# Layer 1's attention scores from half-height stacks on two ranges of rows, and eight maxima of the third group moved to the end of the front

## The reference, cut to what matters

```python
xn = _layernorm(x, axis=-1)
q = _rope(xn @ Wq, cos, sin); k = _rope(xn @ Wk, ...); v = xn @ Wv
k = jnp.repeat(k.reshape(B, S, Hkv, hd), 4, axis=2)     # one key head for four query heads
scores = jnp.einsum('bhqd,bhkd->bhqk', q, k) / jnp.sqrt(jnp.float32(D))
p = jax.nn.softmax(scores, axis=-1)
o = jnp.einsum('bhqk,bhkd->bhqd', p, v)
x = x + o.transpose(0, 2, 1, 3).reshape(B, S, D) @ Wo + slot_ffn(xn)
```

## Time and profile before

| | us |
|---|---|
| median of 3 runs (lowest, highest) | 3282.1 (3274.93, 3283.18) |
| the profiled execution | 3282.72 |
| its span | 3281.0 |
| PE busy | 3021.9 (92%) |
| DVE busy | 1858.9 (57%) |
| ACT busy | 1339.0 (41%) |
| POOL busy | 313.7 (10%) |

### The profile page before, as it was taken

One profiled execution on the slowest core, in us unless ns is written; L12 is line 12 of the kernel. 1 busy time (PEld: TensorE's weight loads), 2 busy tenths in 40 slices (PEclk: granted clock), 3 DMA queues, 4 the chain that ended last, 5 costly groups with the idle time before them and its releaser, 6 DMA issues.

```text
span 3281.0 us, 49871 instructions
## 1 busy us (share of the span) xinstructions
PE 3021.9 (92%) x14086; PEld 1839.2 (56%) x14087; DVE 1858.9 (57%) x4528; ACT 1339.0 (41%) x1921; POOL 313.7 (10%) x349
## 2 busy tenths in 40 slices
PE   5999999999989999999989999999997789989998
PEld 2455545554445555555545555556665466666666
DVE  5655665666547777777637767752223644444552
...
GB/s 205 136 108 80 161 145 107 72 161 148 44 81 49 49 60 61 55 61 55 72 176 32 51 40 37 45 61 76 95 59 66 105 72 91 91 91 85 84 88 18
DMA packets 135433, 276.61 MB, mean 84 GB/s; under 512 B 20144, under 2 KB 77872, under 8 KB 123408
## 3 DMA queue, kind: packets, MB, share of 16 engines
...
## 4 chain that ended last, share of the span: by engine, by line
PE 76%; DVE 9%; issue 5%; ACT 4%; DMA 4%; SPq 1%; another core or an unknown queue 1%; DVEq 0%; POOL 0%; ACTq 0%; POOLq 0%
PE bank L483 7%; PE bank_u L545 6%; PE pair L529 6%; PE pair L585 5%; PE bank L506 5%; PE pair L686 3%; PE pair L1893 3%; PE bank_m L483 3%; PE pair L2718 3%; PE bank_m L2682 3%; PE pair L730 3%; DVE nmax L856 3%; PE bank L2682 3%; PE pair L494 2%; PE pair L2333 2%
## 5 line engine op out<-in xcount | busy, mean ns | idle before, releaser
L762 ACT ACTIVATE probs<-pair 128x1024 f32<-128x1024 f32 x512 | 504.4, 1022 | 260.4 <-PE pair L529 257.3
L856 DVE TENSOR_REDUCE nmax<-bank 128x1 f32<-128x512 f32 x664 | 441.2, 685 | 213.1 <-PE bank L506 209.7
L856 DVE TENSOR_REDUCE nmax<-bank_m 128x1 f32<-128x512 f32 x360 | 246.3, 684 | 86.6 <-PE bank_m L506 81.2
L545 PE MATMUL bank_u<-probs,vext 128*32 128x512 f32 x2048 | 284.5, 629 | 0.3 <-ACT uraw L749 0.3
L506 PE MATMUL bank<-k_a,q_a 96*128 96x512 f32 x336 | 173.4, 551 | 24.5 <-DMA k_a<-parts_dram 21.1
L529 PE MATMUL pair<-q_a,k_a 98*128 98x512 f32 x512 | 171.6, 441 | 17.0 <-ACT probs L762 11.8
L529 PE MATMUL pair<-q,k 98*128 98x512 f32 x512 | 167.2, 410 | 3.2 <-DVEq L1528 2.2
L1928 ACT ACTIVATE probs<-pair 128x896 f32<-128x896 f32 x128 | 115.6, 918 | 122.9 <-PE pair L1815 81.3
L506 PE MATMUL bank<-k,q 96*128 96x512 f32 x328 | 150.4, 493 | 16.7 <-DMA k<-parts_dram 10.6
L2018 DVE CUSTOM_DVE_ANT_0 bank<-bank,mask_q 128x128 f32<-128x128 f32 (+1 forms) x320 | 118.5, 417 | 77.4 <-PE bank L1797 76.4
L529 PEld LDWEIGHTS pair<-q_a,k_a 98*128 98x128 f32 x512 | 88.6, 198 | 112.5 <-ACT probs L762 66.0
...
## 6 DMA issues: line engine op xcount, KB each, us to landing
...
```

The source lines that it names most:

```text
L545: ins = nc.tensor.matmul(bank_u[32 * h:32 * h + 32, :], vext[:, kt, kv(g, h), :], probs[:, kt % 2, h * SEQ:(h + 1) * SEQ], start=(kt == 0) ...
L762: nc.scalar.activation(probs[:, kt % 2, hp * 2 * SEQ:hp * 2 * SEQ + n], st.tile(l, name)[:, 0:n], ACT.Exp).then_inc(st.free["act"].sem, 1)
L856: nc.vector.tensor_reduce(nmax[:, g % 2, qt, h:h + 1], sc.tile(l, name)[:], AX, ALU.max, negate=True).then_inc(sc.free["dve"].sem, 1)
```

## The change

Layer 1's stacks lose their rows of zeros. The even heads of a group now stand on rows 0 to 47 with their maxima on 48 and 49, the odd heads on rows 64 to 111 with theirs on 112 and 113, and each range has its own copy of the keys. So a query stack is half as long (`GH // 2`; a spare buffer keeps the addresses behind it), a stack takes eight transfers instead of four, a load of maxima two instead of one, and the four clears of queries are gone; the two memsets of the key stack set 32 rows each instead of 96 and 2. `score_at` makes neighbours of an even and an odd head, and `two_scores` issues their S together: it waits for both banks, issues both matmuls and signals once. The two E matmuls of a tile lie on different row ranges without being moved.

Of group 2's S, numbers 0 to 7 leave the rounds of the step's own back and are made in the step before, at the end of the front, between the matmuls of the tail. `SHARE1` and the tables are adapted to even numbers.

```diff
--- before.py
+++ after.py
...
 def sc_plan1(front, back):
...
-                    ("back", turn_uses(0) + s_uses(3)[13:] + [("GX", "dve")]),
...
+                    ("back", turn_uses(0) + s_uses(3)[12:] + [("GX", "dve")]),
...
-                    ("back", [("Z2", "act")] + turn_uses(3)))
+                    ("back", [("Z2", "act")]), ("front", s_uses(2)[:2]), ("back", turn_uses(3)), ("front", s_uses(2)[2:8]))
...
-        stack_loaded = [sig(f"stack_loaded{g}", [(64, 0), (64, 0), 0, (64, 0)], "sync") for g in range(GROUPS)]
+        stack_loaded = [sig(f"stack_loaded{g}", [(64, 0), (128, 0), 0, (64, 0)], "sync") for g in range(GROUPS)]
...
-        m_loaded = [sig(f"m_loaded{i}", [(16 - 16 * i, 16 + 16 * i), (16 - 16 * i, 16 + 16 * i), 0, (16 - 16 * i, 16 + 16 * i)], "sync")
+        m_loaded = [sig(f"m_loaded{i}", [(16 - 16 * i, 16 + 16 * i), (32 - 32 * i, 32 + 32 * i), 0, (16 - 16 * i, 16 + 16 * i)], "sync")
                     for i in range(2)]
...
-            return m_loaded[g % 2].at(l, it, 16 * (g // 2 + 1) if g % 2 else 8 * g)
+            return m_loaded[g % 2].at(l, it, (2 if LAYER[l] == 1 else 1) * (16 * (g // 2 + 1) if g % 2 else 8 * g))
+
+        def score_at(l, i):
+
+            return (2 * (i // (2 * TT)) + i % 2, i // 2 % TT) if LAYER[l] == 1 else (i // TT, i % TT)
         def stack_ready(l, it, g):
-            return stack_loaded[g].at(l, it, 0 if g > 1 else stack_loaded[g].per[l])
+            return stack_loaded[g].at(l, it, 0 if g > (2 if LAYER[l] == 1 else 1) else stack_loaded[g].per[l])
...
             name = ("S", g, i)
-            h, qt = i // TT, i % TT
+            h, qt = score_at(l, i)
             dve.wait_ge(*sc.filled(l, it, name))
...
                 if not front:
-                    dve_clear_queries(dve, l, 0)
                     dve_slots(dve, l)
...
-            sp.dma_start(q_rows(g), m_dram[g].rearrange("(a h) n -> a h n", a=2)).then_inc(m_loaded[g % 2].sem, 16)
+            if LAYER[l] == 1:
+                for side in range(2):
+                    sp.dma_start(q_rows(g, side), m_dram[g].rearrange("(a h s) n -> s a h n", a=2, s=2)[side])\
+                      .then_inc(m_loaded[g % 2].sem, 16)
+            else:
+                sp.dma_start(q_rows(g), m_dram[g].rearrange("(a h) n -> a h n", a=2)).then_inc(m_loaded[g % 2].sem, 16)
...
-        q_1 = sb("q_1", [P, GROUPS, GH, SEQ], F32, l1)
+        q_1 = sb("q_1", [P, GROUPS, GH // 2, SEQ], F32, l1)
+        spare_q = sb("spare_q", [P, 8 * SEQ], F32, l1)
...
-            sp.wait_ge(queries_clear, GROUPS)
...
             dve.wait_ge(*st.filled(l, 0, ("E", 0, TT - 1, 1)))
-            nc.vector.memset(k_1[0:96, :, :], 0.0).then_inc(dve_pre1, 1)
-            nc.vector.memset(k_1[96:98, :, :], 1.0).then_inc(dve_pre1, 1)
+            for side in range(2):
+                nc.vector.memset(k_1[64 * side + 32:64 * side + 64, :, :], 1.0).then_inc(dve_pre1, 1)
...
-        def dve_clear_queries(dve, l, g):
-
-            dve.wait_ge(*st.filled(l, 0, ("E", g, TT - 1, 1)))
-            nc.vector.memset(q_1[0:96, g, :, :], 0.0).then_inc(queries_clear, 1)
...
-        SHARE1 = [6, 8, 10, 12, 13, 14, 15, 16, 16]
+        SHARE1 = [6, 8, 10, 12, 12, 14, 14, 16, 16]
...
             def q(g, h):
-                return q_1[0:96, g, h, :]
+                at = h % 2 * 64
+                return q_1[at:at + 48, g, h // 2, :]
             def k(g, h):
-                return k_1[0:96, g, :]
+                at = h % 2 * 64
+                return k_1[at:at + 48, g, :]
             def pair(g, h):
-                return k_1[0:98, g, :], q_1[0:98, g, h, :]
+                at = h % 2 * 64
+                return k_1[at:at + 50, g, :], q_1[at:at + 50, g, h // 2, :]
+
+            def two_scores(g, first, last):
+
+                for i in range(first, last, 2):
+                    if i == 0:
+                        pe.wait_ge(*stack_ready(l, it, g))
+                    for j in range(2):
+                        for s in sc.vacated(l, it, ("S", g, i + j)):
+                            pe.wait_ge(*s)
+                    for j in range(2):
+                        h, qt = score_at(l, i + j)
+                        ins = nc.tensor.matmul(sc.tile(l, ("S", g, i + j))[:], q(g, h)[:, qt * P:(qt + 1) * P].bitcast(F32R),
+                                               k(g, h).bitcast(F32R), start=True, stop=True)
+                    ins.then_inc(sc.full.sem, 2)
             def last_maxima(first, last):
                 if back:
-                    for i in range(first, last):
-                        pe_scores(pe, l, it, 3, i, q, k)
+                    two_scores(3, first, last)
             def project(name, half, weight, width=P, halves=2):
...
             for g in range(GROUPS):
                 for kt in range(TT):
                     cut = SHARE1[2 * kt:2 * kt + 3] if g == 1 else [4 * kt, 4 * kt + 2, 4 * kt + 4]
+                    if g == 0:
+                        cut = [8 + 2 * kt, 10 + 2 * kt, 10 + 2 * kt]
                     if g == 1 and kt == 0 and not front:
                         cut = [0] + cut[1:]
                     def maxima(j):
                         if back if g < 2 else front:
-                            for i in range(cut[j], cut[j + 1]):
-                                pe_scores(pe, l, it, (g + 2) % GROUPS, i, q, k)
+                            two_scores((g + 2) % GROUPS, cut[j], cut[j + 1])
                     if back:
                         pe_scores_t(pe, l, it, g, kt, pair, lambda: maxima(0))
...
                                            start=(k_ == 0), stop=(k_ == 1))
                 ins.then_inc(sc.full.sem, 1)
                 pe_weigh(pe, l, it, GROUPS * TT - 1, kv_of_group)
+            if front:
+                two_scores(2, 0, 2)
+            if back:
                 pe_turn_sums(pe, l, it, GROUPS - 1)
+            if front:
+                two_scores(2, 2, 4)
+            if back:
                 for s in st.vacated(l, it, "OUT"):
                     pe.wait_ge(*s)
                 pe.wait_ge(*done(sc, l, it, "Z2"))
                 for t in range(TT):
                     nc.tensor.matmul(st.tile(l, "OUT")[:, t * DIM:(t + 1) * DIM], alphaT[:, t * P:(t + 1) * P], sv2[:],
                                      start=(t % 2 == 0), stop=False)
+            if front:
+                two_scores(2, 4, 6)
+            if back:
                 pe_turn_heads(pe, l, it)
+            if front:
+                two_scores(2, 6, 8)
+            if back:
                 pe_out_heads(pe, l, it, wo1)
         def act1(act, l, it, step):
...
                 ln_stats(dve, l, it, step, 1)
                 slot_means()
                 dve_values(dve, l, it, None, 4)
-                maxima(2, 0, 2)
+                maxima(2, 8, 10)
                 ln_normalise(dve, l, it, 1)
-                maxima(2, 2, 16)
+                maxima(2, 10, 16)
             if back:
                 maxima(3, 0, 2)
             if front:
...
             if front:
                 low(2, k_parts[:, 1, :], rot_k[:], k_parts[:, 0, :])
             if back:
-                maxima(3, 9, 13)
+                maxima(3, 9, 12)
             if front:
                 route()
             if back:
                 dve_normalise_heads(dve, l, it, step, 0)
-                maxima(3, 13, 16)
+                maxima(3, 12, 16)
             if back:
                 begin_gates()
             if front:
...
                         dve_normalise_heads(dve, l, it, step, g + 1)
                     if front and g == 0 and last == 8:
                         weigh_slots()
+            if front:
+                maxima(2, 0, 2)
             if back:
                 dve_normalise_heads(dve, l, it, step, GROUPS - 1)
+            if front:
+                maxima(2, 2, 8)
+            if back:
                 dve_add_out(dve, l, it)
             step.end()
...
             def stack(g):
                 if BACK[l]:
                     sp.wait_ge(*st.filled(l, it, ("E", g, TT - 1, 1)))
-                heads = slice(GH * g, GH * g + GH)
-                sp_stack(sp, l, it, g, 0, q_1[:, g, :, :], DIM, HD, heads)
-                sp_stack(sp, l, it, g, 1, k_1[:, g:g + 1, :], 64, HD, slice(g, g + 1))
+                for side in range(2):
+                    at = 64 * side
+                    sp_stack(sp, l, it, g, 0, q_1[at:at + 48, g, :, :], DIM, HD, slice(GH * g + side, GH * g + GH, 2))
+                    sp_stack(sp, l, it, g, 1, k_1[at:at + 48, g:g + 1, :], 64, HD, slice(g, g + 1))
             def rows(side, size, at, n):
                 return parts_dram[side, 0:2 * size, :].rearrange("(a f) n -> f a n", a=2)[at:at + n, :, :]
             sp_rounds(sp, l, it, [(rows(0, DIM, 0, P), parts[:, 0, :, :]), (rows(0, DIM, P, P), parts[:, 1, :, :]),
-                                  (rows(1, 64, 0, 64), k_parts[:])], stack, lambda g: q_1[96:98, g, :, :])
```

(1 more changed line is left out.)

11 lines of the change are left out of this document (3 added, 8 removed).

## The result

| | before | after |
|---|---|---|
| median (lowest to highest), us | 3281.35 (3274.93 to 3283.18, 4 runs) | 3306.03 (3301.01 to 3308.76, 4 runs) |
| profiled execution: time, span, us | 3282.72, 3281.0 | 3301.01, 3299.3 |
| mean granted clock over the span | 0.957 | 0.938 |

The ratio is 1.0085, 95% interval 1.0071 to 1.0099: slower, also by the 0.3% that the forecast took as its measure, where 3261.5 us was forecast. The 3306 us also lie above the range. The spans differ by 18.3 us, and layer 1's seven main steps hold nearly all of it: from the first to the last copy of the gate weights on ACT (alphaT, once a step) they take 631.68 us instead of 614.49, +17.2. Layer 1's first copy comes 3.5 us later, and what follows the last one is 2.4 us shorter.

A forecast was written before the change was run, and what follows sets the result against it. PE was taken to pace layer 1's main step, DVE next in line in stage D. From 3282.7 us, seven steps gave -23.8, once-only parts -1.9, +8 and -3.5: -21.2, so 3261.5 us, range 3234 to 3292.

The forecast's parts named there:

- the clock's term in stage D: Start of the last two groups: slow work at 1.2 GHz after a 3 us wait for the stack, +1.5 us a step.
- D: Stage of the last two groups: cheaper pairs, limited by DVE and waits for two banks, -3.3 us a step.
- the clock: Rival, 12%: PE idle in every round, 1.2 GHz returning several times a step; three spells eat 4.9 us; 3285 us.
- I take 0.25: Assumed cost in us of a pair of matmuls on two row ranges, bounded by 0.23 and 0.47; saving 0.22 a pair.
- A: Stage of group 0's weights with group 2's maxima: paired or moved scores, bounded by ACT, -4.0 us a step.
- B and C: Projections, then group 1 up to the next batch's stack: more transfers and loads delay that stack, +1.6 us a step.
- E: Tail and head of the next step: four score pairs added, two hidden, plus array shape switches, +0.8 us a step.
- 2 to 4: Sign: us that PE would wait for the stack at group 0's first score for the maxima in each main step.
- Once-only parts: End of layer 0 -1.9 us, first front of layer 1 +8, last back -3.5.
- One after the other: Rival, 12%: row ranges don't overlap, so a step is 4.2 us longer; 3318 us.
- All of it shows: Rival, 7%: the stack lands no later and DVE keeps up, -10 us a step; 3215 us.
- No spell: Rival, 17%: the forecast without the +1.5 us a step for slow work; 3251 us.

The follow-up runs named there:

- low_rows: Kernel before, same order and single waits, with scores over rows 0 to 47 or 0 to 49 only, all heads on one range: ratio 1.0190.
- tall: The change's order, in twos with both waits, but with the full-height matmuls, stacks and four transfers of the kernel before: ratio 1.0119.
- pad64: The changed kernel with transposed scores over 64 rows of each half instead of 50, the 14 more holding zeros in the queries: ratio 1.0048.
- single_wait: The changed kernel, with each score for the maxima of a pair waiting for its own bank alone and telling DVE by itself: ratio 1.0048.
- move_late: Kernel before with eight of group 2's scores for the maxima moved to the front's end and layer 0's first query clear set behind two copies: ratio 0.9984.
- e_serial: The changed kernel, with both transposed-score matmuls of a tile on one row range, so they run one after the other: ratio 1.0174.
- single64: The single_wait kernel with transposed scores over 64 rows of each half, the 14 more all zeros: ratio 1.0033.

## Why the prediction was wrong

**The step that failed is the clock's term in stage D, "+1.5".** I read one slow stretch behind one wait as one event a step, started by the wait for the stack. The runs show other spells: 13 in the seven steps in place of seven, seven of them 13.7 us long where the one behind that wait had lasted 3.4, and not tied to the stack, for which PE didn't wait in two of the steps that have them. Spells came in both orders: in the good step one fell inside stage C (clock 0.91 there), where it was hidden by the transfer, and the stack's wait was 0.56 us instead of 1.84; in the next it fell into D, 12 us behind the stack's wait. Seven steps cost 17.2 us more than before although a clean one is 2.9 us shorter, so the spells cost (17.2 + 20.5) / 7 = 5.4 us a step, not 1.5. The rival "the clock" had 4.9 us a step, with 12% and 3285; its size was right, its reason (idle time in every round) only half of it. low_rows, tall and pad64 show the other half: the rows taken out of each matmul. The kernel before was granted 2.4 GHz with 48 rows of zeros in each score; I priced these rows at nothing.

**The unit, "I take 0.25".** Full overlap is real, two starts within 0.01 us. The Trainium skill ("TensorE: Matmul & The Clock Gate", Packing small matmuls) puts them some 4 ns apart, and the trace agrees: 3 or 4 ns in most pairs. But the pair's cost to the next kind of matmul is mostly 0.33 us, and I had rows for that reading: E to W took 0.56 for two, 0.09 more than E to E. I used those 0.09 us in the tail alone.

**Stage by stage, at full clock** (forecast, then the good step): A -4.0, -3.9; B and C +1.6, +1.75; D -3.3, -1.9; E +0.8, +1.1. A was bounded by ACT, so the unit did not matter there. In B and C two errors cancel. The eight issues took SP 0.43 us each, as I had said, but each transfer landed some 1.4 us sooner, 2.5 us behind the last issue and not 3.9. And the keys' store came 1.4 us later against the start of B (19.9 us behind it, 18.5 before), 1.0 of it the second load of the maxima, for which I had 0.25. So PE waited 0.56 and 1.84 us for the stack in these two steps and not the 2 to 4 that I had named as a sign. D is the miss of 1.4 us: DVE is 23.8 of 27.2 us busy (87%, as I had said), and PE waits for it seven times, 4.8 us in all. single_wait gets 0.6 of a step back. So a main step without any spell is worth -2.9, not -4.9, and with the forecast's one spell the step would have been 85.4 us, not 83.5. The forecast had -23.8 for the seven steps and +17.2 came: of these 41 us, 2.0 a step, 14 in all, are the sizes, and 3.9 a step, 27 in all, the spells.

**Once-only parts.** The wait at the end of layer 0 shrank from 4.82 to 2.74 us (-2.1, forecast -1.9), and move_late shows the same 2.1 by itself. Layer 1's first S comes 7.8 us earlier, 948.80 and not 956.56. Only 2.1 of it is that wait. Some 4 us were gained ahead of it, where a slow stretch of layer 0 (W at 1.94 us from 875.69) is missing after; the code there is the same, so the change has no part in that, and it is luck. Another 1.3 us comes from a shorter slow stretch right behind the wait. The wait for layer 1's first stack, which I had put at 1.6 us more, was 9.21 us and not 9.56. From the first S of layer 1 to the first copy of the gate weights it takes 35.2 us and not 23.9, +11.3 where my +8 held 4.8 and 2 for it. In the last back E(1) waits 6.00 us for its maxima instead of 0.92:

```profile
1634.16 0.80 PE L533 MATMUL pair<-q,k 50*128 50x512 f32 x2 [6.00 <-DMA q<-m_dram]
```

What stage A gains is lost there, as said; the rest of the kernel is 2.4 us shorter, not 3.5.

**The rivals.** "One after the other" is refuted: the starts coincide. "All of it shows" fell with D and the stack. "No spell" had 3251; with the good step in place of every step it would be 3282.7 - 20.5 and the once-only parts as measured (+1.1), an estimate of some 3263.

**Open.** What exactly the clock gate weighs is not settled: zeros count as rows, 14 more rows help, and work that overlaps helps against the same work in a row (e_serial), but neither idle time nor rows nor work per us puts low_rows, the change and e_serial in order, and I didn't vary columns or data. The changes between full and half height were not tested apart from the rows. The number of spells also differs from run to run (single64 ranges over 35 us), so the single profile of each kernel orders them only roughly. Transfers of group 0's stack on another queue, which would remove the wait of 1.84 us, were not tried.
